# Block 0 of a four-layer residual stack: the order of its two sequences' pieces, and where the first weight splits stand

## The reference

```python
def L0(x):                                   # gated memory
    ctx = causal_ema(x, tau_ctx)
    gated = x * sigmoid(concat([x, ctx]) @ Wg.T + bg)
    mod = 0.5 + sigmoid(gelu(x @ Wn1.T + bn1) @ Wn2.T + bn2)          # one row for each of 16 time constants
    traces = [causal_ema(gated * mod[..., d], tau[d]) for d in range(16)]
    temporal = sum_d softmax(blend)[d] * traces[d]
    soma = gelu(x @ Wsoma.T + bsoma)
    out = (soma * sigmoid(temporal @ Wtemp.T + btemp)) @ Wout.T
    return layernorm(out) * gamma + beta
def L1(x):                                   # masked pooling
    scores = tanh(x @ W1 + b1) @ v
    p = softmax(where(mask[type], scores, -1e30))
    return (p @ x) / cnt
def L2(x):                                   # every token through all 8 experts and a shared one
    g = x @ Wg[e]; u = x @ Wu[e]
    return (1 - sg) * sum_e gate[e] * ((silu(g) * u) @ Wd[e]) + sg * shared(x)
def L3(x):                                   # gelu MLP, a part of its outputs by a chosen expert
    h = gelu(x @ W1 + b1)
    return concat([h @ W2 + b2, h @ We[index] + be[index]])
x = x + L0(x); x = x + L1(x); x = x + L2(x); x = x + L3(x)
```

## Time and profile before

| | |
|---|---|
| device time, median of 3 runs | 2808.72 us |
| profiled execution, first to last instruction | 2807.6 us |
| TensorE matmul busy | 2770.3 us (99%) |
| TensorE weight load busy | 2299.4 us (82%) |
| VectorE busy | 1796.9 us (64%) |
| ScalarE busy | 1449.7 us (52%) |
| GpSimd busy | 1218.6 us (43%) |

### The profile page before, as it was taken

One profiled execution on the slowest core, in us unless ns is written; L12 is line 12 of the kernel. 1 busy time (PEld: TensorE's weight loads), 2 busy tenths in 40 slices (PEclk: granted clock), 3 DMA queues, 4 the chain that ended last, 5 costly groups with the idle time before them and its releaser, 6 DMA issues.

```text
span 2807.6 us, 36696 instructions
## 1 busy us (share of the span) xinstructions
PE 2770.3 (99%) x12794; PEld 2299.4 (82%) x12794; DVE 1796.9 (64%) x2976; ACT 1449.7 (52%) x2625; POOL 1218.6 (43%) x950
## 2 busy tenths in 40 slices
PE   8799999999999999999999999999999999999999
PEld 5678888888888888888888888888888888888888
DVE  8799778867777666556765766555766563333443
ACT  4555666566456544555545644455644563333445
POOL 5256435633554355434543345433454333333334
PEclk9999999999999999999999999999999999999999
DMA  4244333433223322112321222211322131111221
GB/s 154 81 145 125 100 105 104 145 98 102 77 68 99 107 68 68 57 59 69 104 64 59 82 87 74 68 47 57 111 80 66 42 103 45 46 45 46 79 89 58
DMA packets 117383, 230.37 MB, mean 82 GB/s; under 512 B 13672, under 2 KB 58960, under 8 KB 117200
## 3 DMA queue, kind: packets, MB, share of 16 engines
q1 hardware_dynamic: 81808, 190.15, 22.1%
q10 hardware_dynamic: 32832, 29.49, 4.2%
q0 software_dynamic: 2560, 8.39, 1.0%
HBM read 219.89 MB, written 8.09 MB: 81 GB/s over the span
## 4 chain that ended last, share of the span: by engine, by line
PE 93%; DVE 4%; issue 1%; ACT 1%; DMA 0%; SPq 0%; DVEq 0%; ACTq 0%
PE bank L588 20%; PE bank L589 20%; PE bank L590 20%; PE ps_out L588 10%; PE ps_out L590 10%; PE ps_out L589 10%; PE bank L581 1%; DVE trace L1130 1%; DVE trace L1138 1%; DVE w_lo L1210 1%; DVE hid L1244 0%; PE ps_out L581 0%; DMA pre_x<-in_xT 0%; PE bank L709 0%; PE bank L700 0%
## 5 line engine op out<-in xcount | busy, mean ns | idle before, releaser
L1383 POOL TENSOR_TENSOR hid_lo<-hid,hid_hi 128x512 fp32r<-128x512 f32 x640 | 851.0, 1330 | 1532.3 <-ACT hid_hi L1015 1532.0
L588 PE MATMUL bank<-res_lo,w_hi 128*128 128x512 f32 x2432 | 957.1, 394 | 5.7 <-DVE hid L1244 2.6
L589 PE MATMUL bank<-res_hi,w_lo 128*128 128x512 f32 x2432 | 948.6, 390 | 0.0
L590 PE MATMUL bank<-res_hi,w_hi 128*128 128x512 f32 x2432 | 947.4, 390 | 0.0
L1244 DVE TENSOR_TENSOR hid<-hid,bank 128x512 f32<-128x512 f32 x576 | 394.1, 684 | 623.5 <-PE bank L590 597.9
L984 ACT ACTIVATE hid<-bank 128x512 f32<-128x512 f32 x576 | 343.9, 597 | 589.0 <-PE bank L590 588.0
L1210 DVE TENSOR_TENSOR w_lo<-w_raw,w_hi 128x768 fp32r<-128x768 f32 (+2 forms) x520 | 495.0, 954 | 194.3 <-ACT w_hi L946 152.1
L946 ACT ACTIVATE w_hi<-w_raw 128x768 fp32r<-128x768 f32 x392 | 331.3, 845 | 480.5 <-PE ps_out L590 468.5
L588 PEld LDWEIGHTS bank<-res_lo,w_hi 128*128 128x128 f32 x2432 | 457.2, 188 | 99.0 <-issue 4.6
L590 PEld LDWEIGHTS bank<-res_hi,w_hi 128*128 128x128 f32 x2432 | 457.0, 188 | 96.9
L589 PEld LDWEIGHTS bank<-res_hi,w_lo 128*128 128x128 f32 x2432 | 457.4, 188 | 89.7
(11 more groups left out here) (180 smaller groups left out, 1565.4 us busy)
## 6 DMA issues: line engine op xcount, KB each, us to landing
w_raw<-in_chunks SPq DMA_DIRECT2D x392, 384.0 KB
mod_on<-mod_rows ACTq DMA_DIRECT2D x154, 128.0 KB
w_raw<-in_head_chunks SPq DMA_DIRECT2D x64, 224.0 KB
stat<-mod_rows ACTq DMA_DIRECT2D x70, 128.0 KB, 3.2
x_in<-in_xT SPq DMA_DIRECT2D x16, 256.0 KB, 3.8
pre_x<-in_xT SPq DMA_DIRECT2D x14, 256.0 KB, 7.3
soma_rows<-pre_soma SPq DMA_DIRECT2D x14, 256.0 KB, 2.0
soma<-soma_rows SPq DMA_DIRECT2D x14, 256.0 KB, 3.6
```

Of the source, the lines that this page charges most:

```text
L588: mm(out, wh, xl, start=start and i == 0, stop=False, skip_group_check=not lone)
L589: mm(out, wl, xh, start=False, stop=False, skip_group_check=not lone)
L590: last = mm(out, wh, xh, start=False, stop=end, skip_group_check=not lone)
L1383: nc.gpsimd.tensor_tensor(hid_lo[i % DEPTH][:], hid[i % 3][:], f(hid_hi[i % DEPTH][:]), ALU.subtract).then_inc(s_hlo, 1)
```

## The change

Block 0's order is a different one. Up to piece (1,6) it is the same. Then lane 0's traces 5 to 15, pieces (0,12) to (0,22), stand in one run, and after them lane 1's pieces 7 to 46. The pieces of lane 0's tail stand singly after certain pieces of lane 1 (`LEAD_TAIL`): (0,23) and (0,24) after (1,7), (0,27) after (1,8), (0,28) after (1,10), (0,31) after (1,11), (0,33) after (1,12), (0,34) after (1,13), (0,35) and (0,36) after (1,14), (0,38) after (1,15), (0,39) after (1,16), (0,40) after (1,17), (0,41) after (1,18), (0,42) after (1,19), (0,44) after (1,20), (0,46) after (1,21). Lane 1's tail then follows alone.

The splits of chunks 0 to 3 all stand in lane 1's tail: chunk 0 after (1,27), ahead of (1,28); part0 after (1,31); chunk 1 after (1,33), ahead of (1,34); chunk 2 after (1,36) on ScalarE and (1,40) on VectorE; chunk 3 after (1,41) and (1,44).

Lane 1's mixes use the same two banks as lane 0's. Lane 0's variance sum uses its own bank. The accumulator of block b is `home(b)`, that is acc[(b + 3) % 4] in place of acc[b % 4], because the plain side weights still stand in acc[0] to acc[2] when lane 0's residual is written. Nothing is computed that was not computed before, and nothing is left out.

```diff
-TAILS = [(0, 33), (1, 28), (0, 34), (1, 29), (0, 35), (1, 30), (0, 36), (1, 31), (0, 37), (1, 32), (1, 33), (0, 38),
-         (1, 34), (1, 35), (1, 36), (1, 37), (0, 39), (0, 40), (1, 38), (0, 41), (1, 39), (0, 42), (0, 43), (1, 40),
-         (0, 44), (0, 45), (1, 41), (1, 42), (1, 43), (0, 46), (1, 44), (1, 45), (1, 46)]
-
-BESIDE = {(0, 29): [("cut", 0), ("cut_lo", 0)], (0, 30): [("setup", "part0")], (0, 32): [("cut", 1), ("cut_lo", 1)],
-          (1, 33): [("cut", 2)], (1, 37): [("setup", "bias")], (0, 40): [("cut_lo", 2)], (0, 41): [("cut", 3)],
-          (1, 40): [("cut_lo", 3)]}
+LEAD_TAIL = {7: [23, 24], 8: [27], 10: [28], 11: [31], 12: [33], 13: [34], 14: [35, 36], 15: [38], 16: [39], 17: [40],
+             18: [41], 19: [42], 20: [44], 21: [46]}
+
+BESIDE = {(1, 27): [("cut", 0), ("cut_lo", 0)], (1, 31): [("setup", "part0")], (1, 33): [("cut", 1), ("cut_lo", 1)],
+          (1, 36): [("cut", 2)], (1, 37): [("setup", "bias")], (1, 40): [("cut_lo", 2)], (1, 41): [("cut", 3)],
+          (1, 44): [("cut_lo", 3)]}
...
-    for j in range(12, 33):
-        turns0 += [(0, j), (1, j - 5)]
-    turns0 += TAILS
+    turns0 += [(0, j) for j in range(12, 7 + ND)]
+    for j in range(7, PIECES):
+        turns0.append((1, j))
+        turns0 += [(0, x) for x in LEAD_TAIL.get(j, [])]
...
+        def home(b):
+
+            return acc[(b + NACC - 1) % NACC]
...
                     if d == 0:
-                        if not lead:
-                            pe.wait_ge(l_act[s], act_at(s, b, "gate"))
                         pe.wait_ge(l_dve[s], dve_at(s, b, "modpair"))
                         pe.wait_ge(su_dve, su(SETUP_DVE, "small"))
-                    elif not lead:
-                        pe.wait_ge(l_dve[s], dve_at(s, b, f"mul{d - 1}"))
-                    elif d > 1:
+                    if d > 1:
                         pe.wait_ge(l_dve[s], dve_at(s, b, f"mul{d - 2}"))
-                    mm((lead_mix[d % 2] if lead else ps)[:, 0:S], sel[:, d:d + 1].broadcast_to([P, P]), mod_pair[s][:],
+                    elif s:
+                        pe.wait_ge(l_dve[0], dve_at(0, b, f"mul{ND - 2 + d}"))
+                    mm(lead_mix[d % 2][:, 0:S], sel[:, d:d + 1].broadcast_to([P, P]), mod_pair[s][:],
                        start=True, stop=True).then_inc(l_pe[s], 1)
...
-                    if b == 0:
+                    if b == 1:
 
                         done("lo0")
-                        dve.wait_ge(l_pe[1], pe_at(1, 0, "gate"))
-                    TT(acc[b % NACC][:, :, s * S:(s + 1) * S], both, x1[:], ALU.add).then_inc(l_dve[s], 1)
+                    TT(home(b)[:, :, s * S:(s + 1) * S], both, x1[:], ALU.add).then_inc(l_dve[s], 1)
```

More of the change, by code:

```diff
@@ L565, in _ @@
                         sp.wait_ge(s_acc0, CLOSES[x[1]])
-                        sp.dma_start(y_blk[:, 0, b * BT:(b + 1) * BT], acc[b % NACC][:, 0, :]).then_inc(s_y[b % NACC], 16)
+                        sp.dma_start(y_blk[:, 0, b * BT:(b + 1) * BT], home(b)[:, 0, :]).then_inc(s_y[b % NACC], 16)
                     sp.wait_ge(s_acc, CLOSES[x[1]])
                     if b < NBLK - 1:
-                        sp.dma_start(y_blk[:, :, b * BT:(b + 1) * BT], acc[b % NACC][:]).then_inc(s_y[b % NACC], 16)
+                        sp.dma_start(y_blk[:, :, b * BT:(b + 1) * BT], home(b)[:]).then_inc(s_y[b % NACC], 16)
                     else:
-                        sp.dma_start(y_blk[:, 1, b * BT:(b + 1) * BT], acc[b % NACC][:, 1, :]).then_inc(s_y[b % NACC], 16)
+                        sp.dma_start(y_blk[:, 1, b * BT:(b + 1) * BT], home(b)[:, 1, :]).then_inc(s_y[b % NACC], 16)
             for i in range(NACC):
@@ L676, in side @@
                     if b == 0:
-                        pe.wait_ge(l_act[s], act_at(s, b, "sq" if lead else "cen"))
-                        last = plain_sum((lead_mix[0] if lead else ps)[:, 0:S],
+                        pe.wait_ge(l_act[s], act_at(s, b, "cen"))
+                        last = plain_sum(ps[:, 0:S],
                                          [(f(mean_w[:]), gated[s][:, h, :]) for h in range(DH)])
@@ L898, in side @@
                     act.wait_ge(l_pe[s], pe_at(s, b, "var"))
-                    activate(stat[s][:], (lead_mix[0] if lead else ps)[:, 0:S], ACT.Sqrt, bias=eps[:]).then_inc(l_act[s], 1)
+                    activate(stat[s][:], ps[:, 0:S], ACT.Sqrt, bias=eps[:]).then_inc(l_act[s], 1)
                 elif j == 38:
@@ L965, in split @@
                         tok = slice(s * S, (s + 1) * S)
-                        activate(res_hi[slot][:, :, tok], acc[b][:, :, tok], ACT.Copy).then_inc(s_rhi, 1)
+                        activate(res_hi[slot][:, :, tok], home(b)[:, :, tok], ACT.Copy).then_inc(s_rhi, 1)
                     return
@@ L972, in split @@
                         act.wait_ge(s_gate, FINAL_HEAD[b - 2] + 1)
-                activate(res_hi[slot][:], acc[b % NACC][:], ACT.Copy).then_inc(s_rhi, 1)
+                activate(res_hi[slot][:], home(b)[:], ACT.Copy).then_inc(s_rhi, 1)
             def front(i):
@@ L1130, in side @@
                         last = STT(tr[:, h, :], gated[s][:, h, :], bl[:, h, d:d + 1],
-                                   (lead_mix[d % 2] if lead else ps)[:, 0:S], ALU.mult, ALU.mult)
+                                   (ps if b else lead_mix[d % 2])[:, 0:S], ALU.mult, ALU.mult)
                     last.then_inc(l_dve[s], 1)
@@ L1225, in split @@
                     dve.wait_ge(s_rhi, 1)
-                    TT(res_lo[slot][:, :, tok], acc[b][:, :, tok], f(res_hi[slot][:, :, tok]), ALU.subtract)
+                    TT(res_lo[slot][:, :, tok], home(b)[:, :, tok], f(res_hi[slot][:, :, tok]), ALU.subtract)
                     tok = slice(S, 2 * S)
                     dve.wait_ge(s_rhi, 2)
-                    TT(res_lo[slot][:, :, tok], acc[b][:, :, tok], f(res_hi[slot][:, :, tok]),
+                    TT(res_lo[slot][:, :, tok], home(b)[:, :, tok], f(res_hi[slot][:, :, tok]),
                        ALU.subtract).then_inc(s_rlo, 1)
@@ L1234, in split @@
                 split_no[0] += 1
-                TT(res_lo[slot][:], acc[b % NACC][:], f(res_hi[slot][:]), ALU.subtract).then_inc(s_rlo, 1)
+                TT(res_lo[slot][:], home(b)[:], f(res_hi[slot][:]), ALU.subtract).then_inc(s_rlo, 1)
             split_no = [0]
@@ L1249, in back @@
                     return
-                X = acc[b % NACC]
+                X = home(b)
                 if last_close.get(b):
```

## The result

The changed kernel takes 2826.74 us (median of 4 runs, 2824.79 to 2829.00) against 2808.72 us; the ratio is 1.0059, with an interval of 1.0047 to 1.0071. It is slower by 0.5 to 0.7%. The forecast had the sign and the mechanism and was short of the size: 11.9 us forecast, 16.6 us by the ratio (13.2 to 19.9), 18.0 us by the medians. In the later sessions the kernel before had medians of 2810.5 to 2810.7 us, 2 us above the 2808.72 of this one, so the ratio is the better measure. 2826.74 is 0.7 us above the upper end of the range, 2826.0. The profiled execution of the changed kernel took 2825.82 us for a span of 2824.0 us, which is 16.4 us more than the span before. So 1.8 us lie around a span; the prediction had taken 1.1 us, from a median that was not the profiled execution's own time.

What follows compares the result with a forecast made beforehand. VectorE's traces, then a handover chain, set step 0; TensorE-bound work behind it is fixed. 94.1 + 1.9 + 31.2 + 3.0 = 130.2 us for step 0, 11.9 us later than before, gives 2820.6 us; range 2814 to 2826 us.

Steps and rivals of the forecast that it cites:

- The account of VectorE's idle time: Ahead of step 0: VectorE's work stays the same, so step 0 moves by what VectorE's idle time moves.
- rival B: Lane 1's traces: TensorE becomes the bound, stalls of 5 to 7 us, 2825.5 to 2830 us; chance 0.12.
- A: The forecast case: the tail is latency, so a lone one wastes VectorE, 2815.5 to 2825.5 us; chance 0.72.
- Traces, 2.07 us each, alone or alternating: First stage: successive traces start 2.07 us apart in either order; the 27 left take 55.9 us, to 86.6 us.
- Lane 0's tail brought forward, 7.5 us, and 1.9 us of stalls: Among lane 1's traces: lane 0's tail adds 7.5 us on VectorE, waits 1.9 us (bounds 0 and 4); traces end at 96.0.
- VectorE's work up to step 0 is the same before and after: Both stages ahead of step 0: VectorE's operations take as long in total after the change as before.
- The bare lone tail, 26.4 us: Last scan to step 0: lane 1's chain alone takes 26.4 us, against 30.8 us for both lanes together.
- The splits, 4.8 us: Lone tail: 1.8 us each ahead of product and reciprocal, 1.2 us for part0; 4.8 us together, bounds 3 and 7.
- The clock, 3.0 us with bounds 0 and 7: Lone tail: TensorE's pauses drop its clock to 1.2 GHz, up to 1.6 us per eight-record group; 3.0 us taken.
- Behind step 0, a fixed length: Expert work behind step 0 takes as long as before, within 2 us; over 3 us difference would be wrong.
- C: Lone tail: the chain hides the splits, step 0 at 120.5 us, 2808.5 us, up to 2811; chance 0.06.
- D: Lone tail: splits and clock cost half of what was taken, 2811 to 2815.5 us; chance 0.10.

Runs made afterwards that it cites:

- e6: Changed kernel with the first splits off the lone tail's chain and 31 extra matmuls on constants in that tail: 2814.64 us, ratio 1.0016.
- e2: Changed kernel with the splits moved off the lone tail's chain, chunk 0 behind lane 1's product, chunk 1's low part and part0 behind the residual: 2822.50 us, ratio 1.0044.
- e3: Changed kernel with 40 extra matmuls on constants, which nothing reads, in TensorE's idle places of lane 1's tail: 2818.95 us, ratio 1.0031.
- e8: Kernel before with only the first splits moved to the places they have in the changed kernel: 2815.51 us, ratio 1.0018.
- e10: Kernel of e5 with 12 extra matmuls in place of 6 ahead of lane 0's Wout group: 2804.94 us, ratio 0.9983 against the kernel before.
- e4: Kernel before with 21 extra matmuls on constants between piece (1,22) and step 0, some ahead of lane 1's scores: 2810.03 us, ratio 0.9998.
- e5: Kernel of e1 with 19 extra matmuls on constants, none ahead of lane 1's scores: 2806.01 us, ratio 0.9984 against the kernel before.
- e9: Changed kernel with three of GpSimd's adds for lane 1 (traces 7, 10, 12) cut to one column of each half: 2824.30 us, ratio 1.0049.
- e1: Changed kernel with tails alternating at the end and splits placed as before, lane 0's traces still first: 2808.97 us, ratio 0.9995 against the kernel before.

## Why the prediction was right in kind and short in size

The account of VectorE's idle time held in its main part: the traces stayed VectorE's, and the lone tail left it idle for 22.8 of 36.8 us. The size came out short because two terms were too small. By the median the time even lies in the bracket of rival B, 2825.5 to 2830 us, and by the ratio, 2825.3 us, just inside the top of A's; the mechanism decides for A, as B's stalls of 5 to 7 us were not there. The sum, term by term:

- *Traces, 2.07 us each, alone or alternating.* Right, wherever nothing stood between two traces.
- *Lane 0's tail brought forward, 7.5 us, and 1.9 us of stalls.* The tail itself took 6.8 us of VectorE, from 64.3 - 55.2 us in the first stage less the 2.3 us below. The stalls were 2.1 us, at the places named: (0,31), (0,33) and behind (0,38). **The first step that failed** is the length of the operations there. "VectorE's work up to step 0 is the same before and after" does not hold: three operations, taken from rows where GpSimd was quiet, were moved to where it adds, and took 2.3 us more. The busy time up to step 0 grew by only 1.0 us, from 77.3 to 78.3, because a `w_lo` that had stood beside GpSimd's last add, with 2.02 us, now takes 0.96. That row of the trace before would have shown it; I had put it down as one of four. Traces ended at 98.2 us, not 96.0.

```profile
88.01 2.02 DVE L1210 TENSOR_TENSOR w_lo<-w_raw,w_hi 128x768 fp32r<-128x768 f32 x1
```

- *The bare lone tail, 26.4 us.* Measured 26.0 (e6).
- *The splits, 4.8 us.* Measured 3.8 (e2): the two waits for `w_hi` cost 1.6 us each in place of 1.8, and `part0` with the rest 0.6 in place of 1.2. At the low clock the variance group ended at 113.09 us, and the table load behind `part0` at 113.21, hardly later. At full clock the splits cost 4.1 us (30.1 in e3 against 26.0 in e6).
- *The clock, 3.0 us with bounds 0 and 7.* **The second step that failed**, and the larger: 6.7 us (e3). I took it "nearest to two such groups", though my own list of pauses had four, and the small groups of the chain were slow as well. Nearly the whole tail ran at 1.2 GHz, for which I had put the upper bound.
- *Behind step 0, a fixed length.* Right for these two traces: 2689.0 us against 2689.3. Over all traces it is 2687.5 to 2690.6 us; in e3 1.4 us of it went with the clock of the first matmuls.

With 98.2 us and 26.0 + 3.8 + 6.7 us the sum gives 134.7 us, and step 0 was at 135.0.

Of the rivals, B (TensorE the bound among the traces) fell: it was busy 58.5 of 67.5 us there and made VectorE wait 2.1 us. C (the splits hidden) fell in e8 and e2. D (half the costs) fell with the clock. Of the signs that I had named, the two waits for `w_hi`, a VectorE under 55% busy in the tail (38%), the low clock and the unchanged length behind step 0 were seen. Step 0 was after 125 us but not near 130, and VectorE had gaps among the traces, the four waits above.

Why does the stagger not pay? Alternating tails take 30.8 us for two lanes, a lone one takes 26.0 at its best; at full clock it is 28.5 us for two lanes with their splits (e10) against 30.1 for one with them on its chain (e3). So the second lane's tail was nearly free, riding in the pauses of the first. Moved among the traces, where VectorE is full, it costs its whole VectorE time.

## What to carry to other kernels

Two latency-bound chains are best run beside each other; moving one to a stage in which the shared engine is full turns free work into paid work, and leaves pauses that nothing fills. Price a moved operation by rows in which its new neighbours run, not its old ones, and where a change leaves TensorE with long pauses, price every matmul group of the chain at the lower clock, the small ones too. Splits belong behind the chain's instruction in each in-order queue. Extra matmuls belong in a pause, ended by the time the chain's matmuls are ready: too many delay them (e4), too few leave them at the lower clock (e5).

## What the runs showed of the hardware that I had not expected

- Some of VectorE's operations stand still beside GpSimd's add of 128x512: a `tensor_scalar` on 128x2 took 0.76 us in place of 0.17, and 0.17 again once the add was one column wide in each half (e9). A subtraction with both inputs in SBUF took 2.02 us in place of 0.96. Multiplies with an operand in PSUM, the scans, and a reciprocal with one input in SBUF showed none of it: one on 128x2 that started 0.01 us behind the start of an add kept its 0.17 us (89.74).
- Who starts first matters. The operations that were held had started while the add ran. A product with both inputs in SBUF that started 0.16 us ahead of the add kept its 0.67 us, and the add took 1.63 us in place of 1.27:

```profile
61.34 0.67 DVE L1150 SCALAR_TENSOR_TENSOR trace<-trace,soma 128x512 f32<-128x512 f32 x1
...
61.50 1.63 POOL L1379 TENSOR_TENSOR temporal<-temporal,trace 128x512 f32<-128x512 f32 x1 [0.80 <-DVE trace L1140]
```

- Extra matmuls of no use took 6.7 us off a 36.8 us tail (e3), and with their places right they made the kernel of e10 faster than the one without them (e1).
- Executions of one kernel differ by several us (2808.1 to 2813.5 for the kernel before, over the 63 run beside the experiments; 7.1 us in e4, 2.3 in e10), and they go with the mean granted clock of the whole execution: 26 of the 63 had 0.998 and took 2808.1 to 2809.6 us, the other 37 had 0.996 or 0.997 and took 2810.4 to 2813.5. Where in an execution the clock differs, the record shows only for those with a trace; e8, e4 and the kernel before differ already between 70 and 80 us. No run tests what decides it.
